# Attention: the two maxima matmuls of a chunk side by side, and one reduction over 768 columns for them

## The reference

```python
attn = jnp.einsum('bqd,bkd->bqk', q * scale, k)
rel_h = jnp.einsum('bhwc,hkc->bhwk', qr, Rh)
rel_w = jnp.einsum('bhwc,wkc->bhwk', qr, Rw)
bias = (rel_h[..., :, None] + rel_w[..., None, :]).reshape(B * nh, S, S)
attn = jax.nn.softmax(attn + bias, axis=-1)
out = jnp.einsum('bqk,bkd->bqd', attn, v)
```

## Time and profile before

| | |
|---|---|
| median of 3 runs | 2463.01 us (2457.59 to 2463.38) |
| the profiled execution | 2461.0 us, its span 2459.2 us |
| mean granted TensorE clock | 0.911 of full speed |
| attention's first 50 chunks, ahead of the loop | about 322 to 366 us |
| attention's heads | about 370 to 1645 us |
| experts | from about 1790 us |

### The profile page before, as it was taken

The page is one execution under the profiler, slowest core; times in us unless marked ns, Lnnn a source line. Parts: engine busy times, 40 slices in busy tenths (PEclk is TensorE's granted clock), DMA queues, the critical chain, the costliest instruction groups (busy, mean ns, idle before and its releaser), DMA issues. The chain is left out here.

```text
span 2459.2 us, 43933 instructions
## 1 busy us (share of the span) xinstructions
PE 2101.3 (85%) x12356; PEld 1901.5 (77%) x12356; DVE 1815.9 (74%) x3327; ACT 1659.0 (67%) x2909; POOL 724.9 (29%) x451
## 2 busy tenths in 40 slices
PE   7833259898989899898989889977499999999997
PEld 6822138787878778787878778866399999999997
DVE  5555378797979788797979778746677777777775
ACT  3344308786878687687868778871278777777775
POOL 0020023333434343343434333452012211212211
PEclk9955579998999999899989999998699999999999
DMA  6778783544453553454364454303366766766764
GB/s 206 232 160 201 156 155 83 99 94 87 79 113 67 101 97 81 82 96 98 63 119 77 84 99 94 91 24 125 108 204 211 222 221 208 227 216 210 229 213 119
DMA packets 123414, 335.11 MB, mean 136 GB/s; under 512 B 17648, under 2 KB 56008, under 8 KB 117860
## 3 DMA queue, kind: packets, MB, share of 16 engines
q1 hardware_dynamic: 111888, 312.42, 51.0%
q0 software_dynamic: 10400, 19.87, 3.7%
q10 hardware_dynamic: 960, 0.80, 0.1%
HBM read 269.62 MB, written 63.43 MB: 135 GB/s over the span
## 5 line engine op out<-in xcount | busy, mean ns | idle before, releaser
L901 DVE TENSOR_REDUCE mx<-ps_m 128x1 f32<-128x384 f32 x1196 | 631.0, 551 | 204.3 <-PE ps_m L750 194.7
L849 ACT ACTIVATE p_hi<-ps_s 128x768 fp32r<-128x768 f32 x648 | 528.6, 816 | 266.2 <-PE ps_s L764 265.5
L598 POOL TENSOR_TENSOR p_lo<-p_f,p_hi 128x768 fp32r<-128x768 f32 x216 | 414.9, 1921 | 782.9 <-ACT p_f L855 782.9
L855 ACT ACTIVATE p_f<-ps_s 128x768 f32<-128x768 f32 x648 | 526.1, 812 | 6.7 <-POOL p_lo L598 3.6
L750 PE MATMUL ps_m<-key_hi,query_hi 128*128 128x384 f32 x1230 | 425.4, 353 | 104.8 <-DMA query_hi<-rel_hi_d 85.2
L598 DVE TENSOR_TENSOR p_lo<-p_f,p_hi 128x768 fp32r<-128x768 f32 x432 | 447.8, 1036 | 35.6 <-ACT p_f L855 34.4
L761 PE MATMUL ps_s<-query_hi,key_hi 128*128 128x384 f32 x1296 | 345.1, 348 | 44.2 <-issue 39.3
L1593 ACT CAST w_hi<-w_raw 128x384 fp32r<-128x384 f32 x600 | 290.1, 515 | 133.7 <-PE ps_o L1570 128.0
L1711 DVE TENSOR_TENSOR w_lo<-w_raw,w_hi 128x384 fp32r<-128x384 f32 x600 | 316.3, 555 | 75.0 <-ACT w_hi L1593 74.9
L750 PEld LDWEIGHTS ps_m<-key_hi,query_hi 128*128 128x128 f32 x1230 | 235.6, 193 | 159.0 <-DMA query_hi<-rel_hi_d 48.8
L774 PE MATMUL ps_o<-p_hi,val 128*65 128x384 f32 x1296 | 339.1, 343 | 4.3 <-POOL p_lo L598 4.3
(11 more groups left out here) (209 smaller groups left out, 2892.7 us busy)
## 6 DMA issues: line engine op xcount, KB each, us to landing
w_raw<-w_u SPq DMA_DIRECT2D x200, 576.0 KB, 4.7
query_rest<-rel_lo_d SPq DMA_DIRECT2D x36, 864.0 KB
query_rest<-qk_lo_d SPq DMA_DIRECT2D x36, 576.0 KB
query_rest<-qk_hi_d SPq DMA_DIRECT2D x36, 576.0 KB
rel_lo_d<-out_lo SPq DMA_DIRECT2D x6, 1728.0 KB, 31.8
query_hi<-rel_hi_d SPq DMA_DIRECT2D x12, 864.0 KB, 14.7
v_d<-v_sb SPq DMA_DIRECT2D x6, 1170.0 KB, 7.6
val<-v_d SPq DMA_DIRECT2D x12, 585.0 KB, 5.6
```

What stands on the lines that cost most here:

```text
L598: engine.tensor_tensor(p_lo[r][:], p_f[idx % 2], p_hi[r][:].bitcast(F32), ALU.subtract).then_inc(lo_done(0, idx)[0], 1)
L849: act.activation(p_hi[r][:], ps_s[:, bank:bank + 2, 0:TB], ACT.Exp).then_inc(hi_ok, 1)
L855: act.activation(p_f[idx % 2], ps_s[:, bank:bank + 2, 0:TB], ACT.Exp).then_inc(f_ok, 1)
L901: dve.tensor_reduce(mx[s // TILES][:, s // 3 % 6, col:col + 1], ps_m[:, c, 0:TB], AX.X, ALU.max).then_inc(mx_ok, 1)
```

## The change

PE issues both halves of a chunk next to each other, in the place of half 0, behind one wait for `mx_ok` to reach 2n, so that both reductions of the chunk before are done. The matmul and the wait behind pv go. On DVE `reduce_half` goes: the subtraction comes first, and behind it one `tensor_reduce` over both banks (128 x 768 to 128 x 2), which adds 2 to `mx_ok`. `reduce_both` gets a count of its own, so that the loop can use it too; ahead of the loop it does what it did. Nothing is changed on ACT, POOL and SP.

```diff
@@ PE, head @@
-                        pe.wait_ge(mx_ok, number - 1)
-                        half(tp, s, 0, ps_m)
+                        pe.wait_ge(mx_ok, number)
+                        for c in range(2):
+                            half(tp, s, c, ps_m)
                     if k % TILES == 0:
 
                         pe.wait_ge(acc_a, QBLOCKS * h + k // TILES + 1)
                         pe.wait_ge(acc_d, QBLOCKS * h + k // TILES + 1)
                     if k % TILES < TILES - 1:
                         pv(h, par, k)
-                    if maxima:
-                        pe.wait_ge(mx_ok, number)
-                        half(tp, s, 1, ps_m)
@@ DVE @@
-            def reduce_half(count, s, c):
-                dve.wait_ge(mm_ok, 2 * count + c + 1)
-                col = s % 3 * 2 + c
-                dve.tensor_reduce(mx[s // TILES][:, s // 3 % 6, col:col + 1], ps_m[:, c, 0:TB], AX.X, ALU.max).then_inc(mx_ok, 1)
-
-            def reduce_both(s, ps):
-                dve.wait_ge(mm_ok, 2 * s + 2)
+            def reduce_both(count, s, ps):
+                dve.wait_ge(mm_ok, 2 * count + 2)
                 col = s % 3 * 2
                 dve.tensor_reduce(mx[s // TILES][:, s // 3 % 6, col:col + 2], ps[:, :, 0:TB], AX.X, ALU.max).then_inc(mx_ok, 2)
-                negated(s, s)
+                negated(count, s)
@@ DVE, head @@
-                    if maxima:
-                        reduce_half(number, s, 0)
                     up, idx = unit_at(par, k, LOW_LEAD)
                     if not (last and up != par) and idx % POOL_EVERY < POOL_EVERY - 1:
                         low(dve, UNITS * h + k + LOW_LEAD, up, idx)
                     if maxima:
-                        reduce_half(number, s, 1)
-                        negated(number, s)
+                        reduce_both(number, s, ps_m)
```

More of the change, by code:

```diff
@@ L937, in _ @@
             for s in range(UNITS - SHIFT):
-                reduce_both(s, [ps_m, ps_s[:, 0:2, :], ps_s[:, 2:4, :]][s % 3])
+                reduce_both(s, s, [ps_m, ps_s[:, 0:2, :], ps_s[:, 2:4, :]][s % 3])
             for idx in range(LOW_LEAD):
```

## The result

The changed kernel takes 2532.86 us (median of four, 2532.79 to 2535.04) against 2463.2 us: a ratio of 1.0294, interval 1.0275 to 1.0313, 70 us slower. Its profiled execution took 2532.8 us, its span 2531.1 us.

A forecast was written before the change was run, and what follows sets the result against it. PE was taken to bound the kernel, 1.744 us a unit. Per block 0.86 + 1.11 + 0.64 = 2.61 us, over 33 blocks 86, less 13 swallowed by stalls: 2461 + 73 = 2534 us, range 2495 to 2585.

The forecast's parts named there:

- (1): On DVE, 598 pairs of reductions become 598 single ones: busy time falls by 94 us, worth nothing by itself.
- (2): On PE, the second matmul moves in front of the four pv matmuls and one wait per unit goes: zero.
- (3): At PE's remaining wait, both banks must be read before the next unit's pair, 0.69 us into the unit.
- (4): DVE's subtraction before the reduction makes a three-unit loop of 5.55 us against PE's 5.23: 0.32 us longer every three units.
- the signs named: In timeline and rows: three-unit groups of 5.5 to 5.6 us, PE idle behind DVE near 90 us, reduction mean 944 ns.
- The block's end: Two groups of three units where o_t is copied: 0.86 us more a block.
- the walk: Unit-by-unit reckoning of the disturbed groups: 0.86 us more at o_t's copy, 1.11 more at POOL's joining (12.31 against 11.20).
- The joining: Two groups where POOL joins o_t and takes turns with DVE's subtractions: 1.11 us more a block.
- What the heads' stalls swallow: Existing stalls of 7 to 10 us per head absorb 9.5 and 3.5 us: 86 less 13 gives 73.
- Rival A: Faster: DVE is the real brake and less work on it removes waits; 42 us less, 2419 us; chance 0.05.
- Rival B: No change: PE has queue slack or the loop closes at 5.23, stalls swallow the rest; 2461 within 7; chance 0.05.
- Rival C: Much slower: POOL's next subtraction precedes DVE's at the joining; 3.3 us a block, 2643, or 2588 in half; chance 0.10.

The follow-up runs named there:

- e11: The changed kernel with its one reduction over 2 x 192 columns in place of 2 x 384: 2474.55 us, ratio 1.0063.
- e1: The changed kernel with DVE's 768-column reduction ahead of the subtraction in each unit, not behind it: 2533.47 us, ratio 1.0305.
- e4: The changed kernel with its PE order and subtraction first, but two 384-column reductions in place of one of 768: 2514.77 us, ratio 1.0227.
- e7: The changed kernel with its one reduction over 2 x 288 columns in place of 2 x 384: 2499.27 us, ratio 1.0158.
- e2: The changed kernel with LOW_LEAD = 1, subtracting for the unit one ahead instead of two: 2542.94 us, ratio 1.0332.
- e5: e1 plus one POOL wait: its first subtraction behind a joining waits for DVE's subtraction of the unit before: 2459.97 us, ratio 1.0000.
- e9: The kernel before the change, with the same POOL wait as e5: 2452.10 us, ratio 0.9968.

## Why the prediction was right, point by point

- The bound before. PE at 1.744 us a unit with no gap, and waits behind DVE that are few: right; e11 has 1.75 too, with the reduction at 552 ns in place of 953.
- (1) DVE's smaller load is worth nothing: right. DVE is busy 20 us less on the page and the kernel is 70 slower. The reduction takes 953 ns, not 944, and the subtractions got longer (mean 1084 for 1036), so the 94 us that were reckoned did not come in either.
- (2) The pair side by side is worth nothing on PE: right. With the same order on PE, e1's regular units last 1.74 to 1.76.
- (3) and (4), the loop: right in every term, by the timeline, and shown by e4, e7 and e11 from the side of the reduction and by e1 and e2 from that of the subtraction. A regular group loses 0.33 us; the sum had 0.32. Of the signs named, one failed: PE's idle time behind DVE in the ps_m rows is 54.5 us and not near 90. The 90 are there on PEld, 126.8 us behind DVE in place of 37.0; PE's own rows show less of the same waits, since the row of a matmul is longer than the distance to the next: at 628.71 the row before ends at 628.66 and leaves 0.05, where the weight load idled 0.37.
- The block's end: right, 0.78 us in six units (0.49 in the four around it and 0.29 in the next group) where the walk had 0.86.
- The joining: mechanism right, size off. The walk had 1.11 in six units; the rows give 0.33 + 1.19 = 1.52. The walk had the first subtraction end 0.7 us late and the second 1.5. On the turn shown the first isn't late at all: it is issued ahead of POOL's copy and takes 0.96, and the copy takes 1.35 in place of 0.81. The second takes 2.52 in place of 0.95, 1.57 late, and the group with it lasts 7.13 us (611.58 to 618.71), 1.56 over a regular 5.57. So the walk's 1.5 was right and was not carried through: 5.55 + 1.5 + 5.55 are 12.60 us, not 12.31. A whole block thus loses 2.91 us (the mean of 20 blocks without a head's stall) where the sum had 2.61: 10 us too little over 33 blocks.
- What the heads' stalls swallow: mis-sized the other way, and by about as much. The ten blocks of the loop that hold a head's boundary lose 1.14 us on average, so the stall takes 1.8 us and not 0.86 + 0.32; the first block's o_t copy comes at 405.90 for 406.00, so that block loses nothing at all; and the two blocks with the 3.44 us subtraction of the earlier trace rows ran without that wait, which gave 5 us back. Between the first and the last o_t copy the trace of after is 71.1 us longer (20 x 2.91 + 11.4 + 1.5); 73 was forecast. That the total came within 2 us is in part these two errors meeting.
- Rival A (DVE as the brake): excluded by the result. Rival B: excluded. Rival C was real and did not happen here: at each of the 22 joinings away from a head's stall DVE's waiting subtraction gets in ahead of POOL's next one. What goes with it in the traces is how early POOL's next input is there. On the turn shown its p_f ends at 615.85, 0.03 us behind the end of the add; in e1 it ends at 614.43, 0.60 ahead of the add's end, and POOL goes first. The recorded start doesn't tell the two apart: in the earlier trace rows POOL's next starts at 603.99, 0.03 ahead of its add's end as in e1, and DVE still gets in first. "SBUF — State Buffer", section Who interferes with whom, in the Trainium skill, says that the pair is locked for the whole instruction and that issue order decides. The traces agree on the lock; on the order they agree before (DVE 603.18, POOL 603.99, DVE first) and not in e1 (DVE 614.12, POOL 614.99, POOL first). Rival C's price of 3.3 us a block counted the low clock at every joining; in e1, where POOL goes first at all 22, it follows at 11.
- The sum was made against 2461.0 and the median was 2463.2; neither this nor the 0.3% matters here. The upper end of the range, 2585, was meant as rival C in half the blocks, for which the sum itself gives 2588.

## What to carry to other kernels

Merging two instructions that read two buffers in turn is no change of the count alone: it takes the double buffering away, and a reduction that stands behind another instruction in its queue then holds PE up. Before it is done, draw the loop that it closes (who fills, who reads, what stands between them in each queue) and set its length against the bound engine's; here 5.55 against 5.23 was written in the trace of before. And when an experiment gives back the old time, look at the units before believing in "no effect": e1 removed the whole of one loss and brought on another of the same size. When a fix is added to one kernel (e5), give it to the other as well (e9) before the two are called level.

## What the runs showed of the hardware

- DVE's subtraction, which reads two inputs in SBUF, and an instruction of POOL take turns whole. DVE's waiting subtraction ends 0.82 us after the POOL instruction it waited for (an add or a subtraction of 1.83 to 1.85 us).
- Who goes next when POOL's add ends and DVE's subtraction is waiting: in the traces of the 13 kernels, wherever nothing but its p_f held POOL's next subtraction, DVE went first in all 121 cases in which POOL's next p_f had ended at most 0.19 us ahead of the add's end or later, and POOL in all 80 in which it had ended 0.25 us or more ahead of it. POOL's recorded start is 0.03 us ahead of the add's end in cases of both kinds (603.99 before, 614.99 in e1). This is read off the traces; no run was made to test it, and its reason is open.
- A PE idle time of 2.14 to 2.21 us at e1's 22 joinings was followed by half clock at 11 of them and not at the other 11, at the same length; in the changed kernel idle times of 0.7 to 1.3 us were followed by full clock in the rows shown (0.51 at 618.71).
- The 768-column reduction, in the loop, has the price that the one ahead of it had, within 1%, and frees its waiting matmul 0.06 us behind its end.
